# V's remainder gets one buffer for each row tile in a fused attention and experts kernel

## What is computed

```
q = layernorm(x) @ Wq.T;  k = context @ Wk.T;  v = context @ Wv.T
y = softmax(causal(q @ k.T * SCALE)) @ v              # per head
x = x + tanh(g_xattn) * (y @ Wo.T + bo)
x = x + tanh(g_ffn) * (top-6 of 8 experts + shared expert)(layernorm(x))
```

## Time and profile before

| | us |
|---|---|
| median of 3 runs (lowest to highest) | 1912.54 (1911.65 to 1913.35) |
| the profiled execution's own time | 1914.91 |
| its span, first to last instruction | 1912.9 |
| PE busy in the span | 1797.7 (94%) |
| DVE busy | 1435.0 (75%) |
| ACT busy | 962.2 (50%) |
| POOL busy | 906.9 (47%) |

### The profile page before, as it was taken

One profiled execution on the slowest core, in us unless ns is written; L12 is line 12 of the kernel. 1 busy time (PEld: TensorE's weight loads), 2 busy tenths in 40 slices (PEclk: granted clock), 3 DMA queues, 4 the chain that ended last, 5 costly groups with the idle time before them and its releaser, 6 DMA issues.

```text
span 1912.9 us, 33793 instructions
## 1 busy us (share of the span) xinstructions
PE 1797.7 (94%) x11920; PEld 1495.8 (78%) x11920; DVE 1435.0 (75%) x3125; ACT 962.2 (50%) x2260; POOL 906.9 (47%) x1159
## 2 busy tenths in 40 slices
PE   5888998899896799999999999999999999999999
PEld 5777887788785678888878878877888887888887
DVE  6677777877778877777887777797777778877776
ACT  4877877778777633334443433343424334433332
POOL 2667676777665443434623343353333444333330
PEclk9899999999998799999999999999999999999999
DMA  4777786778778432121132211114122111311111
GB/s 139 137 136 133 145 169 142 154 155 157 153 140 171 108 120 88 45 78 45 56 112 76 67 55 67 56 34 154 45 78 77 45 56 66 121 45 66 45 45 44
DMA packets 300999, 182.83 MB, mean 96 GB/s; under 512 B 210080, under 2 KB 265376, under 8 KB 300832
## 3 DMA queue, kind: packets, MB, share of 16 engines
q1 hardware_dynamic: 300832, 180.69, 38.4%
HBM read 111.43 MB, written 18.87 MB: 68 GB/s over the span
## 4 chain that ended last, share of the span: by engine, by line
PE 67%; DVE 13%; POOL 9%; issue 6%; ACT 2%; DMA 1%; SPq 0%; DVEq 0%; POOLq 0%; ACTq 0%
PE gate_up L1264 32%; PE down L1777 18%; PE bank L768 12%; POOL halves L466 2%; DVE ops_lo L1121 2%; DVE acc L1628 2%; PE scores L869 1%; POOL v_parts L471 1%; POOL hidden L1476 1%; DMA turned<-halves 1%; POOL c_lo L458 1%; POOL newton L83 1%; PE down L1756 1%; DVE stats L598 1%; PE rows_t L758 1%
## 5 line engine op out<-in xcount | busy, mean ns | idle before, releaser
L1264 PE MATMUL gate_up<-xo_hi,ops_hi 128*128 128x512 f32 x1120 | 440.3, 393 | 14.4 <-DVE gated L1240 5.7
L1264 PE MATMUL gate_up<-xo_lo,ops_hi 128*128 128x512 f32 x1120 | 436.7, 390 | 0.0
L1264 PE MATMUL gate_up<-xo_hi,ops_lo 128*128 128x512 f32 x1120 | 436.6, 390 | 0.0
L466 POOL TENSOR_TENSOR halves<-probs,halves 128x384 f16<-128x384 f32 x232 | 216.9, 943 | 105.7 <-ACT halves L568 105.7
L1628 DVE SCALAR_TENSOR_TENSOR acc<-down,scale,acc 128x512 f32<-128x512 f32 x320 | 238.1, 745 | 34.7 <-PE down L1777 34.3
L1264 PEld LDWEIGHTS gate_up<-xo_hi,ops_hi 128*128 128x128 f32 x1120 | 210.6, 188 | 68.2 <-DVE gated L1240 11.1
L574 ACT ACTIVATE probs<-probs,neg_max 128x128 f32<-128x128 f32 (+1 forms) x512 | 229.0, 449 | 47.2 <-DVE neg_max L700 47.0
L1777 PE MATMUL down<-d_hi,h_hi 128*128 128x512 f32 x640 | 249.0, 389 | 0.0
L1777 PE MATMUL down<-d_lo,h_hi 128*128 128x512 f32 x640 | 249.0, 389 | 0.0
L1777 PE MATMUL down<-d_hi,h_lo 128*128 128x512 f32 x640 | 249.0, 389 | 0.0
L1476 POOL TENSOR_TENSOR hidden<-hidden,gated 128x512 f32<-128x512 f32 x120 | 157.4, 1319 | 189.9 <-DVE hidden L1245 170.5
(11 more groups left out here) (184 smaller groups left out, 4267.5 us busy)
## 6 DMA issues: line engine op xcount, KB each, us to landing
g_raw<-in_w_gate SPq DMA_DIRECT2D x40, 512.0 KB, 3.5
u_raw<-in_w_up SPq DMA_DIRECT2D x40, 512.0 KB, 3.5
d_raw<-in_w_down SPq DMA_DIRECT2D x40, 512.0 KB, 3.4
c_in<-in_ctx_t SPq DMA_DIRECT2D x16, 512.0 KB, 4.9
x_in<-in_x SPq DMA_DIRECT2D x16, 512.0 KB, 4.4
x_res<-in_x SPq DMA_DIRECT2D x16, 512.0 KB, 4.1
x_between<-x_res SPq DMA_DIRECT2D x16, 512.0 KB, 3.4
acc<-x_between SPq DMA_DIRECT2D x32, 256.0 KB, 4.4
```

Source lines behind the costliest of these rows:

```text
L466: pool.tensor_tensor(halves[k % HALVES][:, 1, :], probs[k % RING][:], halves[k % HALVES][:, 0, :], ALU.subtract).then_inc(p_lo_made, 1)
L1264: ins = pe.matmul(gu_ps[bank][:], ops[x][:, which, a, c, :], xo[y][:, b, c, :], start=(begins and c == 0 and i == 0), stop=(c == CH - 1 an ...
```

## The change

The remainder gets a list of two buffers, and tile t uses `v_rest[t]`. The second buffer has the old one's place; the first lies in the last 2 KB (a partition) of the space that the experts own. Two waits change: DVE's subtraction of tile t waits for POOL's read of the same tile one sweep back, and SP raises `early_free` after the last `v3_made` instead of after the last `v_done`.

```diff
-    sb("experts_space", [P, 2 * JH * C * S])
+    sb("experts_space", [P, 2 * JH * C * S - D])
+    v_rest = [sb("v_rest0", [P, D])]
     v_parts = [sb("v_parts0", [P, T, 3, D], BF16)]
-    v_rest = sb("v_rest", [P, D])
+    v_rest.append(sb("v_rest1", [P, D]))
...
                     if s == 1 and is_last(i):
-                        sp.wait_ge(v_done, T * B)
+                        sp.wait_ge(v3_made, T * B)
...
-                        pool.tensor_tensor(parts[:, t, 2, :], v_rest[:], parts[:, t, 1, :], ALU.subtract).then_inc(v3_made, 1)
+                        pool.tensor_tensor(parts[:, t, 2, :], v_rest[t][:], parts[:, t, 1, :], ALU.subtract).then_inc(v3_made, 1)
...
-                            act.copy(parts[:, t, 1, :], v_rest[:]).then_inc(v2_made, 1)
+                            act.copy(parts[:, t, 1, :], v_rest[t][:]).then_inc(v2_made, 1)
...
-                            wait(dve, v3_made, n.times(T, t))
-                            dve.tensor_tensor(v_rest[:], bank[t][:], v_parts[n.parity()][:, t, 0, :],
+                            wait(dve, v3_made, n.times(T, t + 1 - T))
+                            dve.tensor_tensor(v_rest[t][:], bank[t][:], v_parts[n.parity()][:, t, 0, :],
                                               ALU.subtract).then_inc(v_rest_made, 1)
```

## The result

The changed kernel takes 1893.4 us, the median of 4 runs (1890.9 to 1893.7), beside 1912.1 for the kernel before in the same session (4 runs, 1911.7 to 1913.4). The ratio is 0.9898, 95% interval 0.9881 to 0.9915: 19 us or 1.0% faster. The prediction was 1887.3, range 1879 to 1899: right in direction, inside the range, 6 us too fast.

A forecast was written before the change was run, and what follows sets the result against it. No engine saturated; a chain over several engines bounds the sweep, v_rest waits reaching PE. Nine sweeps at 1.70 (15.3) plus four at 2.62 (10.5) less 0.6 give 25.2 us; 1912.5 - 25.2 = 1887.3, range 1879 to 1899.

The forecast's parts named there:

- two collisions: DVE's normalise pair against POOL's operations ahead of c_lo: each costs POOL about 0.2 us, so c_lo ends 0.4 later.
- The maxima of head 3: DVE's fourth row maxima: would wait 0.8 us for POOL's halves of head 13, covered by work that ended later before.
- Sweeps -1 and 0: First two sweeps, where PE already waits for c_lo: no gain, the earlier normalise costs 0.6 us together.
- everything behind sweep 13: Sweep 14 has no v_rest wait on PE, and the experts run unchanged, only shifted: no gain or loss.
- rows sweeps: Sweeps 4 to 11, and sweep 1 priced alike: K starts 1.70 us earlier in each, 15.3 us over nine.
- it lies 2.4 above the median of the runs shown, which I carry over: Last step: the profiled 1914.9 us lies 2.4 above the median, so 25.2 is taken from 1912.5, giving 1887.3.
- the plain term: Sweeps 2, 3, 12, 13: 2.62 us gained in each, 10.5 together, expecting the slow clock gone with PE's gap.
- The late transposes: Rival: head 15's transpose behind POOL's burst lands late, at worst 0.5 us a sweep, some 7 us, about 1894; chance 0.06.
- PE wanted it at 313.54, and now at 311.84: Head 15's transpose, issued at 307.76, lands at 310.6 to 312.4; PE now needs it at 311.84, at worst 0.5 late.
- PE takes it all: Rival at K: c_lo is not in the way, so 33 us are gained, 1879; chance 0.07.
- Each normalise stops POOL for its whole length: Rival ahead of c_lo: each normalise blocks POOL 0.546 us, c_lo 1.1 later, gain 15 us, 1897.5; chance 0.15.
- Slower: Rival: the normalise keeps POOL out 3.86 us ahead of c_lo, K starts later, about 27 us lost, 1939; chance 0.04.

The follow-up runs named there:

- e1: The changed kernel with DVE's old wait restored (POOL's read of the previous tile), both buffers kept: 1911.6 us, ratio 0.9998 to the kernel before.
- e2: The changed kernel with SP's old condition for early_free, the last v_done: 1893.5 us, ratio 0.9902 to the kernel before.
- e4: The changed kernel, but DVE's normalise waits until c_lo is made: 1951.6 us, ratio 1.0185 to the kernel before.
- e7: The changed kernel with POOL's third part of V for tile 0 moved behind c_lo, to slot 12: 1889.9 us, ratio 0.9869 to the kernel before.
- e0: The changed kernel run again without any edit, also for a second profile: 1892.5 us, ratio 0.9893 to the kernel before.
- e3: The changed kernel, but PE waits ahead of O of tile 1 for POOL's read of tile 0, DVE does not: 1894.9 us, ratio 0.9907.
- e5: The changed kernel with the normalise cut to 8 of 512 columns, leaving computation out: 1889.2 us, ratio 0.9866 to the kernel before.
- e9: The changed kernel with POOL's third parts of V for both tiles moved to slots 14 and 15: 1876.9 us, ratio 0.9818 to the kernel before.
- e6: The kernel before, one buffer, with DVE's normalise moved ahead of v_rest of tile 1: 1910.3 us, ratio 0.9979 to the kernel before.
- e8: The changed kernel with SP's store of x1 moved from slot 0 to slot 1: 1887.5 us, ratio 0.9873 to the kernel before.

## Why the prediction came out as it did

**The mechanism held, step by step.** DVE's wait went, and e1 shows that it is the whole of the gain. The normalise started with the Newton steps' end and slipped between POOL's operations at two collisions; the residual left PE's waits (5.4 us in 9 before, 7.5 in 12 in e1); `c_lo` took its place. SP's condition and the addresses cost nothing (e1, e2). The maxima of head 3 wait 0.64 us for POOL's halves (they end at 474.44 and DVE starts at 474.61), predicted 0.8, and it is covered.

**The sum, against the profile that it was made from.** The predicted gain of the thirteen sweeps was 25.8 us; before to after the table gives 26.1. Sweeps -1 and 0 lost 1.6 (predicted 0.6), and everything behind sweep 13 lost 0.6 (predicted 0). 26.1 - 1.6 - 0.6 is 23.9, the difference of the two spans, 1912.9 and 1889.0; predicted 25.2. The own times of the two executions differ by 24.1. So the total was nearly right for this pair of executions, and partly by luck: the eight rows sweeps gained 15.7 us where 13.6 were predicted, the four plain ones 8.9 where 10.5 were.

**The step that failed** is the last one: "it lies 2.4 above the median of the runs shown, which I carry over". I took a gain from a disturbed execution and subtracted it from the median. The profile before lies 3.4 us above the median of 13 later runs (1911.55), the profile after 2.5 below its own median. Part of what the change removes is in that execution only: all four plain sweeps ran partly at 1.2 GHz behind the gap, each 0.9 us longer than at full clock (37.9 against 37.0). In e1, whose own time of 1912.1 is typical, only one plain sweep shows it. Hence the plain term, 2.62 for each of four, was right for that profile (37.89 to 35.29 and 37.88 to 35.28 are 2.60), but without the slow clock it is 36.99 - 35.28 = 1.71: with three of four undisturbed about 2.7 us too much for a typical execution.

Only these two executions of the old order have a profile. The mean clocks of the other runs agree in the main: of ten runs of the kernel before, beside e4 to e7, the four above 1915 us had 0.980 to 0.982, and five of the six below 1913.2 had 0.983 to 0.986. But of the 13 beside e0 to e3 the slowest, 1915.8, had 0.984, so the clock isn't all of the spread.

The other half of the 6 us lies in the late transposes and behind sweep 13, both put at nothing in the sum; the rows sweeps made up for part of it. From e1 to e0, with predicted in brackets, the rows sweeps give 16.0 (13.6), the plain ones 5.6 (10.5), sweep 1 1.0 (1.7), sweeps -1 and 0 -0.3 (-0.6), and all behind sweep 13 -2.8 (0).

**The rows sweep was under-sized:** 2.15 us undisturbed (37.55 to 35.40), predicted 1.70. 0.33 of the missing 0.45 is a wait that I had not priced: PE's transposes of the rows for the experts waited for t_lo, 2.6 us in 8 sweeps of e1, none after.

**The late transposes were given no price in the forecast,** only as a rival. They took much of this back. Between 85 and 575 us PE waits 1.7 us (3 times) for them before and 2.3 (3) in e1, but 5.1 (6) after and 5.8 (9) in e0. In the table these are the sweeps of 36.0 to 36.2 and of 36.97 beside those of 35.3 to 35.5. At 0.5 us a sweep the rival's own estimate was 7; 3 to 4 us came. The step "PE wanted it at 313.54, and now at 311.84" used the issue of one sweep and PE's need in it, where the landings vary by more than the margin (2.8 to 4.6 us).

**Behind sweep 13** e0 takes 2.8 us longer than e1, and all of it arises before the experts' stage is under way: 1.2 in sweep 14, from the transposes, 0.6 from transposes in the last sweeps, and 0.9 where the attention ends and the experts begin. There the stretch at the slow clock lasts longer, as the windows of e0 and then of e1 show:

```profile
627.00:634.50 7.50, 5.60 (x22) 4.50 (x23) 3.40 (x5) 0.60 (x1) 3.88 (x3) 0.54 0.69 210
```

```profile
649.00:656.50 7.50, 7.11 (x35) 5.87 (x36) 4.10 (x6) 1.18 (x2) 3.68 (x2) 0.77 0.56 192
```

In the experts the distance stays at 2.7 to 2.8 us, so they do run "unchanged, shifted" here; what failed is taking the end of the attention as unchanged too. From e1 to e0 it is 22.6 - 0.3 - 2.8 = 19.5, the difference of their spans, and of the medians 19.1.

**The rivals.** *PE takes it all* is out: `c_lo` is late in every sweep. *Each normalise stops POOL for its whole length* is out: two collisions cost `c_lo` 0.35 and not 1.1, and leaving them out gives 0.36 (e5). The Trainium skill's page "SBUF — State Buffer", section "SBUF: two separate sides", has the loser blocked for the other's whole instruction; for POOL, as the one that loses, the trace does not bear it out with the recorded shortest duration, 0.546 us, since POOL's operations grew by 0.18 to 0.20. For DVE, as the one that loses, it fits: its pair of normalises takes 2.44 us for 1.1, and ends 0.29 us behind POOL's operation. *Slower* needed a delay of `c_lo` of 2.1 us; it was 0.35.

## What to carry to other kernels

Before a gain is read from one profile, see whether that execution is a typical one: sum a term for disturbed sweeps only as often as other executions have it. The engine at which a wait ends is not the price of it: 20 us of PE's waits hid a chain through the residual, and a wait of 13 us put back on PE cost about 2 (e3). A buffer added to remove a wait also frees the order: moving the read out of the busiest stretch (e9), which one buffer does not allow, gave another 0.75% (14 us) beside the 1.07% (20 us) of the buffer itself, by the ratios of e9 and e0.

## What was not expected of the hardware

- DVE's product `y` (L657, 128x256, two operands in SBUF) took 0.42 us undisturbed and 0.82 at this place in the old order, but 2.04 in the new one, where it is issued at 469.61 during `c_lo` and ends at 471.65, 0.28 us behind the end of `c_lo` at 471.37. That looks like a wait until POOL's operation is over, recorded as duration; the pair of normalises ends as close (0.29) behind POOL's operation. It was covered, because K needs only the first residual.
- The slow clock came only behind some gaps. Of the 13 gaps ahead of O, those of 1.3 to 1.65 us were never followed by it, before, in e1 or in e6; those of 1.75 to 1.8 were in four of five sweeps (before) and one of five (e1); those of 1.9 and 2.0 in five of six (e6). Gaps of 3.3 to 3.8 ahead of K came with it in all 13 (e4), gaps of up to 1.2 in e3, and of up to 1.4 in the changed kernel between 85 and 575 us, in none. Late transposes leave such gaps as well: those of 1.9 to 2.3 us in sweep 14 were followed by it in e2, e5 and e7, one of 2.4 in e8 was not. In the kernel before it made a plain sweep 0.9 us longer. Why the same gap is followed by it in one execution and not in another is open.
